# An attention loop's order of work: scores for the row maxima 1.5 steps ahead in place of 2, projections and loads rearranged

## Chip, cores and metric

One Trainium2 chip, one core. The metric is the device time of one execution in microseconds, the median of several runs. The kernel before takes 815.4 us (median of 3 runs, 815.37 to 815.62).

## What is computed

A macaron block on x of shape (8, 512, 128) in float32, 4096 tokens: half a feed-forward block, attention, and half a feed-forward block again. The feed-forward block (`_L0_ffn_ref`: 64 routed experts, the best 8 of a token, 64 places each, and a shared expert) isn't touched by the change. The attention, cut to what matters:

```python
def _L0_attn_ref(x, wq, bq, wk, bk, wv, bv, wo, bo, gamma, beta):
    B, S, E = x.shape            # 8, 512, 128
    H = 16; D = 8
    Q = (x @ wq + bq).reshape(B * H, S, D)
    K = (x @ wk + bk).reshape(B * H, S, D)
    V = (x @ wv + bv).reshape(B * H, S, D)
    scores = jnp.einsum('bqd,bkd->bqk', Q, K) / jnp.sqrt(jnp.float32(D))
    attn = jax.nn.softmax(scores, axis=-1)
    ctx = jnp.einsum('bqk,bkd->bqd', attn, V).reshape(B, S, E)
    out = ctx @ wo + bo + x
    out = layernorm(out) * gamma + beta
    return out

x = x + 0.5 * _L0_ffn_ref(_layernorm(x), ...)
x = x + _L0_attn_ref(_layernorm(x), ...)
x = x + 0.5 * _L0_ffn_ref(_layernorm(x), ...)
```

`Q.reshape(B * H, S, D)` reads rows of x in order, so 32 tokens (a row of 128 values is 16 positions of a head) are one head of 512 positions. A tile of 128 tokens therefore holds 4 whole heads.

## The kernel before

The program is one stream per engine (`block.sync`, `gpsimd`, `vector`, `scalar`, `tensor`), each in the order written, with semaphores between them. It is feed-forward, attention, feed-forward. The attention goes over NT = 32 tiles of 128 tokens; **step n** does tile n, and beside it pieces of later and earlier tiles. In the trace the steps run from about 225 us to 632 us.

What a step n does, by engine:

- **TensorE** (`step`, from line 1755; a loop body for the middle steps and written out for the first and last four). 16 positions `tau` in 4 quarters. Each issues `scores_t` (line 1743), the transposed scores of tile n for one block of keys and one head, into one of two PSUM banks; it waits for the exponential two positions before. At tau 1, 5, 9 and 13 come two calls of `scores` each (lines 1728 and 1730, part p of 8), plain scores of tile n+2 that only serve the row maxima; each waits for the maximum two parts before (`a_mx`). After tau 3, 7, 11 and 15 comes `pv` (line 1752, four heads side by side, each as several matmuls), which is the value product of the quarter before. Between them stand `xT` (line 1687, transpose for tile n+4), `qk` (1692, query and key projection for n+4), `v` (1701, value projection for n+3), `maxT` (1710, transpose of the maxima of n+1) and `proj` (1718, output projection of n-2). These five share PSUM bank 7 in turn: the list `uses` fixes their order, and each waits until the one before it was read.
- **ScalarE** exponentiates each `scores_t` (line 1453) and copies out `xT` (1393, after tau 1), `maxT` (`max_copy`, 1408, after tau 3), the value product (`ctx_copy`, 1414, after tau 3) and `qk` (1400, after tau 7).
- **VectorE** reduces the 8 parts of plain scores of tile n+2 to maxima (`row_max`, 1122), then splits them in two bf16 halves (`max_high` 1126, `max_low` 1130), and between them does `v_copy` (845), the reciprocal of `ctx_div` (1135), `z_add` (1146) and layer norm pieces. Some steps in every four have more of those.
- **GpSimd** multiplies the context by the reciprocal (`context`, 784), splits queries and keys in three bf16 parts (`split`, 759 to 765) and normalises the next tile.
- **SyncE** issues all DMAs of the loop from one queue, in order. `stack_load(n+3)`: 16 DMAs (lines 472 to 484) that bring the parts of tile n+3 back from DRAM as stacks of rows; it waits until those parts have landed in DRAM (`a_pst`) and until step n-1 has issued its last `scores_t`. `max_rows(n+1)` (458): the transposed maxima into two rows of the query stack, which the first `scores_t` of step n+1 needs (`a_mrow`). `ctx_store(n-1)` (498), 256 KB to DRAM. `stack_store(n+4)` (463), 192 KB to DRAM, once `split` is done (`a_parts`). `ctx_load(n-1)` (506): two DMAs that read the context back; it waits until `ctx_store(n-1)` has landed.

The wait that `ctx_load` has, and the wait of a stack load (`wait_each` is the helper at line 96 of the profile):

```python
wait_each(sp, (a_use, use("o", t - 2) + 1 if ... else 0), (a_cst, 16 * t + 16))   # ctx_load(t)
wait_each(sp, (a_ST, 16 * (t - 3)), (a_pst, 16 * t + 16))                         # stack_load(t)
```

Of the kernel before, what the change touches and what calls it, by code (L numbers as in the profile page):

```python
# [15 lines left out]
def macaron_kernel(nc, x_in, wq, bq, wk, bk, wv, bv, wo, bo, gamma, beta,  # L16
# [10 lines left out]
    NT = T // P  # L27
# [24 lines left out]
    NBUF = 4  # L52
    NPB = 8
    AW = 19072
    assert NH * HS == P and C * 2 == P and T % (P * GT) == 0
# [9 lines left out]
    with ExitStack() as ctx:  # L65
# [284 lines left out]
        for n in range(NT + 2):  # L350
            uses += [u for u in (("x", n + 4), ("m", n + 1), ("q", n + 4), ("v", n + 3), ("o", n - 2))
                     if 0 <= u[1] < NT]
# [16 lines left out]
        def _(sp):  # L369
# [84 lines left out]
            def attention():  # L454
# [40 lines left out]
                def ctx_store(t, r):  # L495

                    sp.wait_ge(a_cx, t + 1)
                    sp.dma_start(ctx_dram[r], ctx_r[r % 2]).then_inc(a_cst, 16)
# [28 lines left out]
                def step(n, r, end=NT):  # L527
                    mid = not isinstance(n, int)
                    if mid or n + 3 < end:
                        stack_load(n + 3, (r + 3) % NBUF)  # L530
                    if mid or n + 1 < end:
                        max_rows(n + 1, (r + 1) % NBUF)
                    if mid or n >= 1:
                        ctx_store(n - 1, (r - 1) % NBUF)
                    if mid or n + 4 < end:
                        stack_store(n + 4, r)
                    if mid or n >= 1:
                        ctx_load(n - 1, (r - 1) % NBUF)
                def store_tokens(g):
# [289 lines left out]
        def _(dve):  # L829
# [285 lines left out]
            def attention():  # L1115
# [42 lines left out]
                max_low(0, 0)  # L1158
                for p in range(8):
                    row_max(1, 1, p)  # L1160
                max_high(1, 1)
                max_low(1, 1)

# [42 lines left out]
                for n in range(NT):  # L1206
                    r = n % NBUF
                    at = lambda k: (r + k) % NBUF
                    for p in range(8):
                        if n + 2 < NT:  # L1210
                            row_max(n + 2, at(2), p)
                        if p == 0 and n >= 6 and n % GT == 2:
# [7 lines left out]
                        if p == 3 and n >= 7 and n % GT == 3:  # L1220
                            x_add((n - 7) // GT)
                        if p == 4 and n + 3 < NT:
                            v_copy(n + 3, at(3))
# [4 lines left out]
                        if p == 7 and n >= 7 and n % GT == 3:  # L1228
                            x_var((n - 7) // GT)
                        if n == NT - 2 and p == 1:  # L1230
                            xT_copy(0)
# [7 lines left out]
                        if n == NT - 1 and p == 4:  # L1239
# [3 lines left out]
                            routed(1)  # L1243
                    if n + 2 < NT:
                        max_high(n + 2, at(2))
                        max_low(n + 2, at(2))
                    if n >= 2:
# [39 lines left out]
        def _(act):  # L1287
# [102 lines left out]
            def attention():  # L1390
# [55 lines left out]
                for n in range(NT):  # L1446
                    r = n % NBUF
                    for tau in range(16):
# [5 lines left out]
                        if tau == 1 and n + 4 < NT:  # L1454
                            xT_copy(n + 4, r)
                        if tau == 3 and n + 1 < NT:
                            max_copy(n + 1, (r + 1) % NBUF)
                        if tau == 3 and n >= 1:
                            ctx_copy(n - 1, (r - 1) % NBUF)
                        if tau == 7 and n + 4 < NT:  # L1460
                            qk_copy(n + 4, r)
# [50 lines left out]
        def _(pe):  # L1512
# [165 lines left out]
            def attention():  # L1678
# [77 lines left out]
                def step(n, r, end=NT):  # L1756
                    mid = not isinstance(n, int)
                    at = lambda k: (r + k) % NBUF
                    for tau in range(16):
                        if tau == 0 and (mid or n + 4 < end):  # L1760
                            xT(n + 4, r)
                        if tau == 6 and (mid or n + 4 < end):
                            qk(n + 4, r)
                        if tau == 10 and (mid or n + 3 < end):
                            v(n + 3, at(3))
                        if tau == 14 and (mid or n >= 2):
                            proj(n - 2, at(-2))
                        if not mid and n == NT - 2 and tau == 2:
                            pe.wait_ge(a_mx, 8 * NT)
                            transposes(ffns[1], 0, 0)  # L1770
                        if not mid and (n, tau) in ((NT - 2, 10), (NT - 1, 2), (NT - 1, 10)):
                            g = 2 * (n - (NT - 2)) + tau // 8
                            transposes(ffns[1], g, g % 2)
                            logits(ffns[1], g - 1, (g - 1) % 2)
                        scores_t(n, r, tau)
                        if tau == 3 and (mid or n + 1 < end):
                            maxT(n + 1, at(1))
                        if tau == 3 and (mid or n >= 1):
                            pv(n - 1, at(-1), 3)
                        if tau % 4 == 3 and tau > 3:  # L1780
                            pv(n, r, tau // 4 - 1)
                        if tau % 4 == 1 and (mid or n + 2 < end):
                            scores(n + 2, at(2), tau // 2)
                            scores(n + 2, at(2), tau // 2 + 1)

# [10 lines left out]
                for p in range(8):  # L1796
# [10 lines left out]
                    scores(0, 0, p)  # L1807
                for p in range(8):
                    scores(1, 1, p)
                    if p == 0:  # L1810
                        maxT(0, 0)
# [50 lines left out]
```

## Time and profile before

| | |
|---|---|
| median of 3 runs | 815.4 us (815.37 to 815.62) |
| the profiled execution's own time | 816.08 us |
| its span, first to last instruction | 813.9 us |
| busy in the span: PE, DVE, ACT, POOL | 79%, 74%, 56%, 50% |
| mean granted TensorE clock | 0.833 of full speed |
| step 13, first `scores_t` | 391.94 us |
| step 17, first `scores_t` | 442.69 us |

The clock column of the profile's 40 slices stands at full speed (9) from the thirteenth slice to the thirty-second, which is the attention after its start. The engines' own busy times overlap; SyncE has none, since issuing a DMA isn't counted as work, though its queue is busy with it. The steps come in groups of four: of these the first is 12.4 us long and the other three a little longer, since VectorE has more to do in them.

### The profile page before, as it was taken

Reading aid. Unit: us, or ns where it says so; the run is one execution under the profiler, and the core shown is the slowest. Engines: PE = TensorE matmul, PEld = TensorE weight load, DVE = VectorE, ACT = ScalarE, POOL = GpSimd, SP = SyncE. Lnnn points to the kernel's source line nnn. Section 1 sums busy time; section 2 is a strip of 40 time slices with the busy share of each in tenths; the row PEclk is TensorE's granted clock in tenths of the full one; section 3 lists DMA queues with packets and bytes.
Section 4 is the critical chain, followed back from the end, with each engine's and each line's share of the span. In section 5 each row is a group of like instructions: output and inputs, shape, how many; then the busy total and the mean of one; then the engine's idle time right before and its main releaser. Section 6 shows DMA issues by size and latency. Waiting matters only on the chain.

```text
span 813.9 us, 16314 instructions
## 1 busy us (share of the span) xinstructions
PE 646.0 (79%) x5121; PEld 283.7 (35%) x5121; DVE 599.6 (74%) x1550; ACT 458.5 (56%) x1057; POOL 408.8 (50%) x559
## 2 busy tenths in 40 slices
PE   4896577632699999999999999999999776667760
PEld 3643455421222222222222232222223533445540
DVE  4788834446878989999899998999983779844430
ACT  5653222210158878888888888888888544222220
POOL 5576778854523234344343443434211448578763
PEclk9997755665579999999999999999999568755665
DMA  7898444325544454454545545455421213443334
GB/s 197 235 252 230 94 75 65 52 24 144 96 87 115 100 116 122 104 128 104 123 113 111 122 102 125 111 112 122 104 58 40 68 29 92 110 88 67 60 42 116
DMA packets 242983, 86.66 MB, mean 106 GB/s; under 512 B 169992, under 2 KB 235688, under 8 KB 242856
## 3 DMA queue, kind: packets, MB, share of 16 engines
q1 hardware_dynamic: 226048, 73.05, 37.8%
q0 software_dynamic: 12288, 10.49, 8.7%
q10 hardware_dynamic: 4584, 2.39, 1.0%
q8 instruction: 25, 0.41, 0.2%
q14 instruction: 38, 0.31, 0.1%
HBM read 56.23 MB, written 31.49 MB: 108 GB/s over the span
## 4 chain that ended last, share of the span: by engine, by line
PE 30%; DVE 26%; POOL 13%; issue 13%; ACT 7%; DMA 7%; SPq 1%; ACTq 0%; POOLq 0%; DVEq 0%
DVE arena L1122 14%; PE psum L1752 8%; PE psum L1743 8%; POOL sums L692 7%; ACT arena L1453 4%; DMA sums<-sums_sb,sidx 4%; POOL arena L667 4%; PE psum L1728 4%; DVE arena L1135 3%; PE psum L1533 2%; DMA arena<-dispatch_rows,arena 1%; DVE arena L1130 1%; PE psum L1692 1%; DVE arena L939 1%; PE psum L1550 1%
## 5 line engine op out<-in xcount | busy, mean ns | idle before, releaser
L1122 DVE TENSOR_REDUCE arena<-psum 128x2 f32<-128x1024 f32 x256 | 306.0, 1212 | 36.3 <-PE psum L1730 36.3
L1453 ACT ACTIVATE arena<-psum 128x512 f32<-128x512 f32 x512 | 278.3, 598 | 72.1 <-PE psum L1743 71.2
L1743 PE MATMUL psum<-arena 122*128 122x512 bf16 x512 | 164.4, 387 | 7.0 <-ACT arena L1453 3.5
L1752 PE MATMUL psum<-arena 128*32 128x512 f32 x1024 | 138.2, 610 | 0.0
L692 POOL DMA_INDIRECT sums<-sums_sb,sidx x64 | 102.0, 1594 | 41.2 <-issue 19.4
L1728 PE MATMUL psum<-arena 48*128 48x512 bf16 x256 | 88.4, 400 | 17.0 <-DMA arena<-qk_parts 7.9
L784 POOL TENSOR_TENSOR arena<-arena 128x128 f32<-128x128 f32 x30 | 14.0, 466 | 149.5 <-DVE arena L1135 149.5
L1730 PE MATMUL psum<-arena 48*128 48x512 bf16 x256 | 88.4, 401 | 0.0
L1743 PEld LDWEIGHTS psum<-arena 122*128 122x128 bf16 x512 | 42.7, 100 | 130.1 <-ACT arena L1453 123.5
L667 POOL DMA_INDIRECT arena<-dispatch_rows,arena x64 | 64.1, 1002 | 27.9 <-issue 17.9
L1610 PE MATMUL psum<-ident,arena 128*128 128x128 f32 x64 | 25.0, 413 | 54.6 <-DMA arena<-dispatch_rows,arena 54.5
L1048 DVE COPY sums_sb<-psum 128x256 f32<-128x256 f32 x32 | 13.6, 425 | 65.8 <-PE psum L1654 44.8
L1728 PEld LDWEIGHTS psum<-arena 48*128 48x128 bf16 x256 | 19.2, 94 | 85.5 <-DVE arena L1122 46.3
L1361 ACT ACTIVATE arena<-psum 128x256 f32<-128x256 f32 x32 | 12.3, 384 | 63.1 <-PE psum L1610 63.1
L1367 ACT ACTIVATE arena<-psum 128x192 f32<-128x192 f32 x32 | 10.6, 331 | 65.5 <-PE psum L1620 65.5
L1620 PE MATMUL psum<-wgu_sb,arena 128*32 128x192 f32 x512 | 45.1, 498 | 0.9 <-ACT arena L1361 0.9
L759 POOL CAST arena<-arena 128x256 bf16<-128x256 f32 x30 | 14.6, 487 | 41.8 <-issue 30.0
L1610 PEld LDWEIGHTS psum<-ident,arena 128*128 128x128 f32 x64 | 10.4, 171 | 71.6 <-issue 46.1
L1040 DVE TENSOR_TENSOR arena<-arena,psum 128x192 f32<-128x192 f32 x32 | 11.3, 353 | 27.5 <-ACT arena L1367 27.5
L1752 PEld LDWEIGHTS psum<-arena 128*32 128x32 f32 x1024 | 20.6, 108 | 31.3 <-issue 31.2
L1533 PE MATMUL psum<-rwT,z_sb 128*128 128x64 f32 x128 | 28.3, 397 | 3.8 <-ACT z_sb L1477 3.8
L1135 DVE RECIPROCAL arena<-arena 128x128 f32<-128x128 f32 x32 | 30.1, 942 | 0.0
(152 smaller groups left out, 1178.9 us busy)
## 6 DMA issues: line engine op xcount, KB each, us to landing
ctx<-arena SPq DMA_DIRECT2D x32, 256.0 KB, 2.1
arena<-qk_parts SPq DMA_DIRECT2D x127, 64.0 KB
qk_parts<-arena SPq DMA_DIRECT2D x32, 192.0 KB, 3.8
arena<-qk_parts SPq DMA_DIRECT2D x190, 32.0 KB
arena<-qk_parts SPq DMA_DIRECT2D x63, 96.0 KB
arena<-lists SPq DMA_DIRECT2D x16, 256.0 KB, 3.5
sums<-x_sb SPq DMA_DIRECT2D x16, 256.0 KB, 4.6
arena<-ctx SPq DMA_DIRECT2D x64, 64.0 KB, 2.4
```

Source lines behind the costliest of these rows:

```text
L667: pool.indirect_dma_start(out=gat[k % NGB], out_offset=None, in_=xw_dram[f.p], in_offset=bass.IndirectOffsetOnAxis(ap=gidx[:, k:k + 1], ax ...
L692: pool.indirect_dma_start(out=acc_dram[f.p], in_=sum_r[q % 2][:, j * D:(j + 1) * D], in_offset=None, out_offset=bass.IndirectOffsetOnAxis( ...
L1122: dve.tensor_reduce(mx_r[r % 2][:, p:p + 9:8], src, X, ALU.max).then_inc(a_mx, 1)
L1135: dve.reciprocal(den2_r[r % 2], den2_r[r % 2]).then_inc(a_rc, 1)
L1453: act.activation(p_r[tau % NPB], bank[4 + tau % 2][:, :], ACT.Exp, scale=SCALE).then_inc(a_P, 1)
L1533: ins = pe.matmul(bank[2 + r][:, j * E:(j + 1) * E], xT_all[:, t * P:(t + 1) * P], rwT[:], start=True, stop=True)
L1610: ins = pe.transpose(bank[0][:, j * P:(j + 1) * P], gat[k % NGB][:, 0:D], ident[:])
L1620: ins = pe.matmul(bank[2 + r][i * HC:(i + 1) * HC, j * 2 * F:(j + 1) * 2 * F], gT[r][:, j * P + i * HC:j * P + (i + 1) * HC], wgu_sb[:, e, :],
L1728: pe.matmul(bank[2 * p % 4][:, :], heads(q_st[r], low, g)[:, cols], heads(k_st[r], low, g), start=True, stop=True, tile_position=(0, 0))
L1730: pe.matmul(bank[2 * p % 4 + 1][:, :], heads(q_st[r], high, g)[:, cols], heads(k_st[r], high, g + 2), start=True, stop=True, tile_position ...
L1743: pe.matmul(bank[4 + tau % 2][:, :], keys, heads(q_st[r], rows, g), start=True, stop=True)\
L1752: ins = pe.matmul(bank[6][32 * g:32 * g + 32, :], v_r[r][:, g, kt, :], p_r[(4 * kt + g) % NPB], start=(kt == 0), stop=(kt == 3), tile_posi ...
```

## The change

- TensorE computes plain scores for the maxima 1.5 tiles ahead (`HEAD = 4`): in step n the last four parts of tile n+1 and then the first four of n+2, where it was eight of n+2. The start-up does only four parts of tile 1.
- `qk` moves from tau 6 (inside a quarter) to tau 4 (before the quarter's first `scores_t`); `v` moves from before tau 10 to after tau 7, next to `pv`; `maxT` moves from tau 3 to tau 11. `uses` follows.
- ScalarE: `max_copy` after tau 10 in place of 3, `qk_copy` after tau 4 in place of 7.
- VectorE: the last half of a tile's maxima comes first, `max_high` and `max_low` follow after part 3 of a step; `v_copy` after that.
- SyncE: `ctx_store`, `ctx_load`, `max_rows`, `stack_store` in place of `max_rows`, `ctx_store`, `stack_store`, `ctx_load`.
- In the last two steps the first transposes for the second feed-forward block stand later.

The sizes and the number of instructions in a step stay.

```diff
+    HEAD = 4
...
-            uses += [u for u in (("x", n + 4), ("m", n + 1), ("q", n + 4), ("v", n + 3), ("o", n - 2))
+            uses += [u for u in (("x", n + 4), ("q", n + 4), ("v", n + 3), ("m", n + 1), ("o", n - 2))
...
                     if mid or n + 3 < end:
                         stack_load(n + 3, (r + 3) % NBUF)
+                    if mid or n >= 1:
+                        ctx_store(n - 1, (r - 1) % NBUF)
+                        ctx_load(n - 1, (r - 1) % NBUF)
                     if mid or n + 1 < end:
                         max_rows(n + 1, (r + 1) % NBUF)
-                    if mid or n >= 1:
-                        ctx_store(n - 1, (r - 1) % NBUF)
                     if mid or n + 4 < end:
                         stack_store(n + 4, r)
-                    if mid or n >= 1:
-                        ctx_load(n - 1, (r - 1) % NBUF)
...
-                for p in range(8):
+                for p in range(HEAD):
                     row_max(1, 1, p)
-                max_high(1, 1)
-                max_low(1, 1)
...
                     for p in range(8):
-                        if n + 2 < NT:
-                            row_max(n + 2, at(2), p)
+                        ahead, part = divmod(HEAD + p, 8)
+                        if n + 1 + ahead < NT:
+                            row_max(n + 1 + ahead, at(1 + ahead), part)
+                            if part == 7:
+                                max_high(n + 1 + ahead, at(1 + ahead))
+                                max_low(n + 1 + ahead, at(1 + ahead))
...
-                        if p == 4 and n + 3 < NT:
+                        if p == 3 and n + 3 < NT:
                             v_copy(n + 3, at(3))
...
-                        if tau == 3 and n + 1 < NT:
+                        if tau == 10 and n + 1 < NT:
                             max_copy(n + 1, (r + 1) % NBUF)
...
-                        if tau == 7 and n + 4 < NT:
+                        if tau == 4 and n + 4 < NT:
                             qk_copy(n + 4, r)
...
-                        if tau == 6 and (mid or n + 4 < end):
+                        if tau == 4 and (mid or n + 4 < end):
                             qk(n + 4, r)
-                        if tau == 10 and (mid or n + 3 < end):
-                            v(n + 3, at(3))
...
                         scores_t(n, r, tau)
-                        if tau == 3 and (mid or n + 1 < end):
+                        if tau == 7 and (mid or n + 3 < end):
+                            v(n + 3, at(3))
+                        if tau == 11 and (mid or n + 1 < end):
                             maxT(n + 1, at(1))
...
-                        if tau % 4 == 1 and (mid or n + 2 < end):
-                            scores(n + 2, at(2), tau // 2)
-                            scores(n + 2, at(2), tau // 2 + 1)
+                        if tau % 4 == 1:
+                            ahead, p = divmod(HEAD + tau // 2, 8)
+                            if mid or n + 1 + ahead < end:
+                                scores(n + 1 + ahead, at(1 + ahead), p)
+                                scores(n + 1 + ahead, at(1 + ahead), p + 1)
```

SyncE's queue, the end of one step and the start of the next. Before, from the last load of a stack on (`L482` a key load, `L458` max_rows, `L498` ctx_store, `L463` stack_store, `L506` ctx_load, `L472` the first load of the next stack):

```order
L482 DMA arena<-qk_parts 8x4x512
L458 DMA arena<-arena 2x16x128 [waits a_misc_read]
L498 DMA ctx<-arena 128x512 [waits a_ctx_copied]
L463 DMA qk_parts<-arena 128x24x32 [waits a_parts_ready]
L506 DMA arena<-ctx 128x4x32 [waits a_ctx_stored,a_misc_written]
L506 DMA arena<-ctx 128x4x32
L472 DMA arena<-qk_parts 24x4x512 [waits a_parts_stored,a_scoresT_in_psum]
```

And with the change, whose lines are numbered one higher:

```order
L483 DMA arena<-qk_parts 8x4x512
L499 DMA ctx<-arena 128x512 [waits a_ctx_copied]
L507 DMA arena<-ctx 128x4x32 [waits a_ctx_stored,a_misc_written]
L507 DMA arena<-ctx 128x4x32
L459 DMA arena<-arena 2x16x128 [waits a_misc_read]
L464 DMA qk_parts<-arena 128x24x32 [waits a_parts_ready]
L473 DMA arena<-qk_parts 24x4x512 [waits a_parts_stored,a_scoresT_in_psum]
```

The context's store now has its reload right behind it, and the maxima's rows and the store of the parts stand behind that reload; nothing is left between the parts' store and the load that waits for its landing.

TensorE's second quarter of a step in the loop. Before (`L1743` scores_t, `L1728` and `L1730` plain scores, `L1692` qk, `L1750` and `L1752` pv):

```order
L1743 MATMUL psum<-arena 128x512 [waits a_exp_ready]
L78 REGISTER_ALU
L1728 MATMUL psum<-arena 128x512 [waits a_max_ready]
L1730 MATMUL psum<-arena 128x512
L78 REGISTER_ALU
L1692 MATMUL psum<-arena,wqk_sb 128x128 [waits a_misc_read]
L1692 MATMUL psum<-arena,wqk_sb 128x128
L78 REGISTER_ALU
L1743 MATMUL psum<-arena 128x512 [waits a_exp_ready]
L78 REGISTER_ALU
L1743 MATMUL psum<-arena 128x512 [waits a_exp_ready]
L1750 REGISTER_ALU [waits a_ctx_copied,a_exp_ready]
```

With the change (`L1742` scores_t, `L1727` and `L1729` plain scores, `L1700` v, `L1749` pv's wait):

```order
L1727 MATMUL psum<-arena 128x512 [waits a_max_ready]
L1729 MATMUL psum<-arena 128x512
L79 REGISTER_ALU
L1742 MATMUL psum<-arena 128x512 [waits a_exp_ready]
L79 REGISTER_ALU
L1742 MATMUL psum<-arena 128x512 [waits a_exp_ready]
L79 REGISTER_ALU
L1700 MATMUL psum<-wv_sb,arena 32x32 [waits a_misc_read]
L1700 MATMUL psum<-wv_sb,arena 32x32 x15
L1749 REGISTER_ALU [waits a_ctx_copied,a_exp_ready]
```

The projection no longer stands between the plain scores and the quarter's last two `scores_t`; these now follow the plain scores at once, and the value projection comes after them.

## Rows read from the trace of the kernel before

**Rows 1.** Page, part 1: busy time of each engine over the span.

```profile
PE 646.0 (79%) x5121; PEld 283.7 (35%) x5121; DVE 599.6 (74%) x1550; ACT 458.5 (56%) x1057; POOL 408.8 (50%) x559
```

**Rows 2.** Timeline of PE; columns: start, duration in us, engine, line.

```profile
391.94 0.60 PE L1743 MATMUL psum<-arena 122*128 122x512 bf16 x2
392.47 0.39 PE L1728 MATMUL psum<-arena 48*128 48x512 bf16 x1
...
392.70 0.38 PE L1728 MATMUL psum<-arena 48*128 48x512 bf16 x1
...
393.01 0.88 PE L1743 MATMUL psum<-arena 122*128 122x512 bf16 x2
...
398.52 0.39 PE L1728 MATMUL psum<-arena 48*128 48x512 bf16 x1
...
399.03 0.39 PE L1728 MATMUL psum<-arena 48*128 48x512 bf16 x1
...
442.69 0.38 PE L1743 MATMUL psum<-arena 122*128 122x512 bf16 x1
...
594.37 0.60 PE L1743 MATMUL psum<-arena 122*128 122x512 bf16 x2
```

**Rows 3.** Timeline of SyncE's DMA queue, one step; columns as in rows 2.

```profile
392.18 0.31 SPq L472 DMA_DIRECT2D arena<-qk_parts  x1
...
398.28 0.64 SPq L458 DMA_DIRECT2D arena<-arena  x1
398.95 0.42 SPq L498 DMA_DIRECT2D ctx<-arena  x1
401.06 0.38 SPq L463 DMA_DIRECT2D qk_parts<-arena  x1
401.54 2.14 SPq L506 DMA_DIRECT2D arena<-ctx  x2
...
404.85 0.31 SPq L472 DMA_DIRECT2D arena<-qk_parts  x1
```

**Rows 4.** Waits of SyncE's queue, 300 to 640 us: total us, times, longest.

```profile
SPq L463 <- POOL arena L765: 31.1, 21, 2.7
SPq L96 <- DMA qk_parts<-arena: 23.7, 23, 1.4
SPq L96 <- DMA ctx<-arena: 14.4, 15, 1.7
```

**Rows 5.** Line 463 (stack_store), 300 to 640 us: us from issue to landing.

```profile
DMA to landing us min/median/max: 3.7/3.8/4.3
```

**Rows 6.** Line 498 (ctx_store), same stretch.

```profile
DMA to landing us min/median/max: 2.0/2.1/2.7
```

**Rows 7.** SyncE's queue late in the loop, no stack in flight.

```profile
609.93 0.34 SPq L498 DMA_DIRECT2D ctx<-arena  x1
612.00 0.92 SPq L506 DMA_DIRECT2D arena<-ctx  x2
```

**Rows 8.** SyncE's queue in step 0 and the start of step 1.

```profile
235.12 0.68 SPq L458 DMA_DIRECT2D arena<-arena  x1
...
240.97 0.30 SPq L472 DMA_DIRECT2D arena<-qk_parts  x1
```

**Rows 9.** Timeline of ACT in step 13.

```profile
392.36 1.09 ACT L1453 ACTIVATE arena<-psum 128x512 f32<-128x512 f32 x2 [0.60 <-PE psum L1743]
...
397.85 0.63 ACT L1400 ACTIVATE arena<-psum,bqk_sb 128x128 f32<-128x128 f32 x2
398.41 1.08 ACT L1453 ACTIVATE arena<-psum 128x512 f32<-128x512 f32 x2
```

**Rows 10.** Windows: length, busy us of PE, PEld, DVE, ACT, POOL; PE clock, DMA.

```profile
225.00:235.00 10.00, 9.24 (x32) 2.37 (x30) 6.73 (x8) 5.17 (x12) 0.29 (x1) 0.51 0.45 100
241.00:595.00 354.00, 345.40 (x2909) 101.29 (x2911) 325.08 (x480) 291.39 (x634) 137.94 (x269) 1.00 0.50 114
...
620.00:640.00 20.00, 15.80 (x90) 7.52 (x89) 12.37 (x71) 12.97 (x34) 7.34 (x12) 0.85 0.18 48
```

More of the change, by code:

```diff
@@ L1229, in attention @@
                             x_var((n - 7) // GT)
-                        if n == NT - 2 and p == 1:
+                        if n == NT - 2 and p == 4:
                             xT_copy(0)
@@ L1243, in attention @@
                             routed(1)
-                    if n + 2 < NT:
-                        max_high(n + 2, at(2))
-                        max_low(n + 2, at(2))
                     if n >= 2:
@@ L1761, in step @@
                             xT(n + 4, r)
-                        if tau == 6 and (mid or n + 4 < end):
+                        if tau == 4 and (mid or n + 4 < end):
                             qk(n + 4, r)
-                        if tau == 10 and (mid or n + 3 < end):
-                            v(n + 3, at(3))
                         if tau == 14 and (mid or n >= 2):
                             proj(n - 2, at(-2))
-                        if not mid and n == NT - 2 and tau == 2:
+                        if not mid and n == NT - 2 and tau == 9:
                             pe.wait_ge(a_mx, 8 * NT)
                             transposes(ffns[1], 0, 0)
-                        if not mid and (n, tau) in ((NT - 2, 10), (NT - 1, 2), (NT - 1, 10)):
+                        if not mid and (n, tau) in ((NT - 2, 14), (NT - 1, 2), (NT - 1, 10)):
                             g = 2 * (n - (NT - 2)) + tau // 8
@@ L1807, in attention @@
                     scores(0, 0, p)
-                for p in range(8):
+                for p in range(HEAD):
                     scores(1, 1, p)
```

## Prediction

> **What bounds the kernel now.** I read the page first. PE is busy for 79% of the span and DVE for 74% [rows 1], which doesn't say what limits a step, so I went to the timelines of one stretch, steps 13 to 16. Their first `scores_t` stand at 391.94 and 442.69 [rows 2], so four steps take 50.75 us and one takes 12.69 on average. The whole loop runs with TensorE at its full clock, 2.4 GHz over 241 to 595 us [rows 10].
>
> In PE's timeline the reader is to see two small stalls. The first `scores_t` of a quarter starts at 391.94, its exponential only at 392.36, and a pair of exponentials takes 1.09 [rows 9]. The third `scores_t` therefore can't start before about 393.0, and the fourth follows the second exponential at 393.5, which is why the row at 393.01 lasts 0.88 where a pair takes 0.60 [rows 2]. The other stall is DVE's: two parts of plain scores start 0.51 apart (398.52 and 399.03), where a part takes 0.23 (392.47 to 392.70 [rows 2]), so PE waited 0.28 for a maximum. Steps with more work on DVE are longer than 12.42, the length of step 13, and 12.69 - 12.42 = 0.27 is what that costs on average. All that a perfect removal of the maxima's wait could give is so 0.28 + 0.27 = 0.55 us a step.
>
> Then the queue that has no busy time on the page, SyncE's [rows 3]. It issues 16 stack loads from 392.18 on, the maxima's rows at 398.28, the context's store at 398.95, then waits for `split` and stores the parts at 401.06, reloads the context at 401.54 (2.14 long), and issues the next stack load at 404.85, which is when the parts' store has landed. Over 300 to 640 us this last wait occurs 23 times for 23.7 us [rows 4]. One turn of the queue is 12.67 here, against a step of 12.69: **the queue is already as long as the step**, with one free place in it, the wait for `split` (31.1 us over 21 times [rows 4], 1.5 a turn). In the present order two landings lie under other things: the context's 2.1 under that wait for `split`, and 2.5 of the parts' 3.8 under the reload.
>
> **The change, part by part.**
>
> *SyncE's order.* No DMA is added or removed, but each landing now stands bare. One turn:
> - 16 stack loads: 392.18 to 398.28 [rows 3], 6.10.
> - `ctx_store` to the start of `ctx_load`, which now waits for its landing right behind it: 2.07 where nothing else is in flight [rows 7]; the landing has a median of 2.1 and reaches 2.7 [rows 6]. I take 2.15, the median and a short gap.
> - `ctx_load`: 0.92 when the queue is quiet [rows 7], against 2.14 behind the parts' store [rows 3]. It is quiet now. With the gap 0.96.
> - `max_rows`: 398.28 to 398.95, 0.67.
> - `stack_store` to the next stack load: 401.06 to 404.85, 3.79; landings are 3.7 to 4.3 [rows 5].
>
> The sum is 6.10 + 2.15 + 0.96 + 0.67 + 3.79 = 13.67; I use 13.7. The low end is 13.5 (2.07, and 3.7 for the landing), the high end about 14.7 (2.7 and 4.3). I stay near the low end, since the parts' store will find only the two small reloads ahead of it, and stores that followed another transfer by a second or more landed in the median time. What is ready is ready: `split` ends about 9 us into a step (401.06 - 391.94), the store now comes 9.9 into the turn, and the copy of the maxima after tau 10 comes about 9 us into a step that began before the turn did.
>
> The Trainium skill, "DMA: Bandwidth & Descriptors", section "Anatomy of one DMA", fits a DMA's time as 2.0 us and its bytes over 436 KB per us, measured for GpSimd's path. By it the 192 KB store would take 2.45 and the 256 KB one 2.6, and the turn 12.8. The trace disagrees for the 192 KB store, which lands in 3.8 [rows 5]; its runs are of 64 bytes.
>
> *Who waits for the queue.* `max_rows(n+1)` stands 9.2 us into the turn (6.10 + 2.15 + 0.96) and the first `scores_t` of step n+1 waits for its landing. Its landing isn't listed; the nearest rows are landings of 2.0 to 2.1 [rows 6, 7], and I take 2.1. So step n+1 starts 11.3 after turn n began. Turn n+1 begins 13.7 after turn n, and nothing in it waits for the engines: from the first turns on, a step takes a turn, 13.7, also the steps in which DVE has more to do. The stacks themselves aren't late; they have half a step more.
>
> *The total.* Turn 1 begins at 240.97 now [rows 8]. With the change `split` for tile 4 is earlier, since step 0 no longer waits behind four parts of scores, so the store follows `max_rows` (235.12 + 0.67 = 235.79), and turn 1 begins at 235.79 + 3.79 = 239.6. There are 27 turns with a store in them (n from 1 to 27). Step 29 starts at 239.6 + 27 x 13.7 + 11.3 = 620.8 in place of 594.37 [rows 2]: 26.4 us later. For the last three steps and the second feed-forward block I take no difference: they have no stack to load, and the transposes that move a few positions there are followed by work that waits for other things. **The sum is +26.4 us.** It is made against the profiled execution, 816.08 by its own time (span 813.9 and 2.2 around it), which is 0.7 above the median. Against the median it is 815.4 + 26.4 = 841.8, and I say 842.
>
> *PE's and ACT's order.* Beside that the engines' own path gets longer, but less. In the second quarter `qk` stood between the plain scores and the third `scores_t` and covered the exponential's 1.06 us (0.41 to its start, 0.60 and a gap). Now `qk_copy` (0.56 in ACT's stream: 397.85 to 398.41 [rows 9]) falls between the quarter's first and second exponential. The fourth `scores_t` can start 0.42 + 0.49 + 0.56 + 0.60 + 0.05 = 2.12 after the first, where its place in PE's order is 0.27 x 3 + 0.45 = 1.26 (three `scores_t` at half of 392.47 - 391.94 each, two parts of scores at 0.23): a stall of 0.86. In the third quarter the same holds without the copy, 1.56 against 1.26: 0.3, which `v` covered. Of the 0.55 for DVE's waits I let 0.5 go, since the reciprocal and the extra pieces get no longer and the maxima have half a tile more room. So 0.86 + 0.3 - 0.5 = +0.66 a step, to 13.35, below the turn of 13.7. It hides under the queue; were the queue short, it would be the cost.
>
> **Rivals.**
> - *The queue doesn't bind, the engines' order does.* It would be so if the landings came faster when nothing follows them. Step 13.35: 27 x 0.66 = 17.8 later, less about 1 at the start, 832. Against it: a turn of 13.35 needs every piece below its least row. By the Trainium skill's fit above (a turn of 12.8) this is what would happen. Chance 0.11.
> - *Faster.* If SyncE's turn also hid (below 12.2) and the exponential's stalls were covered by `pv`, only the gain would be left: 0.55 a step, 27 x 0.55 = 15 less, 800; halved, 808. The point from which it decides is a turn of 12.69. For it: 15 waits for the context's landing are short already [rows 4]. Against it: the two landings alone are 5.9 of a turn now. Chance 0.03, and 0.02 that both halves cancel within 0.2%.
> - *The clock falls.* PE will stand idle for some 1 to 2 us at the start of a step. In 620 to 640 us it was busy for 15.80 of 20 us and the clock went down to 0.85 on average; at 225 to 235 it was 0.51, that is 1.2 GHz, with PE busy for 9.24 of 10 us [rows 10]. At half clock a step's 11 us of matmuls would be longer than any turn; step by step that is 5 us or more each, and three such steps 15 more, 857. The Trainium skill, "TensorE: Matmul & The Clock Gate", section "HAM oscillation", says that DMA waits within a matmul loop can take the clock down again and again. By that rule it would be 857 or more. Here PE stays busy for over 80% of each step with short gaps only. Chance 0.04.
>
> **The numbers.** The forecast, a step of one turn of 13.5 to 14.2, has 0.80: 836 to 856. The range 833 to 856 takes in the turn's likely values and touches the engines-only case. A measurement of this kernel tells about 0.2% from no change. Slower by more: 0.80 + 0.11 + 0.04 = 0.95; same 0.02; faster 0.03.
>
> **What would show it.** Right: first `scores_t` of steps 13.7 apart with no difference between the four kinds of step; SyncE's queue never waiting for `split`, waiting 1.7 a turn for the context's landing and 3.4 for the parts'; PE's wait before a step's first `scores_t` put down to the DMA of the maxima's rows; the clock at 1.00 throughout. Wrong: steps of four different lengths, waits for `split` still there, or the next stack load starting less than 3.7 after the store.

## The result, and the profile after

The changed kernel takes 860.0 us (median of 4 runs, 854.0 to 860.8) against 815.51 us for the kernel before on the same chip: a ratio of 1.0512, 95% interval 1.0462 to 1.0561. The direction and the mechanism of the prediction hold; the time lies above the range (833 to 856). The profiled execution took 854.0 us by its own time (span 852.0), so the rows below explain 38 of the 44.5 us; the other executions are told of with the first experiment. Two more executions on record took 853.8 and 859.07: they lie near 854 or near 860.

The chain that ended last, as shares of the span by engine, of the kernel before:

```profile
PE 30%; DVE 26%; POOL 13%; issue 13%; ACT 7%; DMA 7%; SPq 1%; ACTq 0%; POOLq 0%; DVEq 0%
```

and of the changed kernel:

```profile
DMA 23%; SPq 19%; issue 14%; PE 13%; DVE 13%; POOL 13%; ACT 4%; POOLq 0%; ACTq 0%; DVEq 0%
DMA qk_parts<-arena 10%; POOL sums L692 7%; DMA ctx<-arena 5%; SPq L473 5%; SPq L483 4%; POOL arena L667 4%; DVE arena L1122 3%; DMA sums<-sums_sb,sidx 3%; SPq L485 3%; SPq L475 3%; PE psum L1751 3%; PE psum L1742 3%; SPq L507 2%; ACT arena L1452 2%; PE psum L1532 2%
```

TensorE and VectorE had 56% of the chain and now have 26%; SyncE's queue and the DMAs had 8% and now have 42%. The busy time of PE barely moved, which is why the first part of the page says nothing of this loss:

```profile
PE 646.1 (76%) x5121; PEld 280.6 (33%) x5121; DVE 610.0 (72%) x1550; ACT 466.6 (55%) x1057; POOL 406.1 (48%) x559
```

It answers to [rows 1]. Next, one turn of SyncE's queue in the changed kernel (timeline: start, duration, engine, line), which answers to [rows 3]:

```profile
479.48 0.31 SPq L473 DMA_DIRECT2D arena<-qk_parts  x1
...
485.58 0.35 SPq L499 DMA_DIRECT2D ctx<-arena  x1
487.70 0.93 SPq L507 DMA_DIRECT2D arena<-ctx  x2
488.67 0.63 SPq L459 DMA_DIRECT2D arena<-arena  x1
489.34 0.41 SPq L464 DMA_DIRECT2D qk_parts<-arena  x1
493.17 0.31 SPq L473 DMA_DIRECT2D arena<-qk_parts  x1
```

The loads take 6.10, the context's store to its reload 2.12, the reload 0.97, the maxima's rows 0.67, the parts' store to the next load 3.83: 13.69 in all, where the prediction had 13.67. The waits of SyncE's queue over 300 to 615 us (total, times, longest):

```profile
SPq L97 <- DMA qk_parts<-arena: 65.6, 22, 3.6
SPq L97 <- DMA ctx<-arena: 41.6, 23, 2.8
SPq L459 <- DVE z_sb L1146: 1.1, 2, 0.6
```

The wait for `split`, 31.1 us in [rows 4], is gone, and the two landings have grown from 23.7 and 14.4 to 65.6 and 41.6. TensorE's own rows show who waits at the other end. The first is the start of step 13, the second of step 17, the others of steps 18 and 29 (in brackets the idle time ahead and what ended it):

```profile
406.98 0.39 PE L1742 MATMUL psum<-arena 122*128 122x512 bf16 x1
...
463.35 0.60 PE L1742 MATMUL psum<-arena 122*128 122x512 bf16 x2
...
477.00 0.60 PE L1742 MATMUL psum<-arena 122*128 122x512 bf16 x2 [0.30 <-DMA arena<-arena]
...
630.27 0.64 PE L1742 MATMUL psum<-arena 122*128 122x512 bf16 x2 [2.29 <-DMA arena<-arena]
```

`DMA arena<-arena` is the transfer of the maxima's rows. Steps 13 to 16 last 56.37 us, 14.09 each, against 12.69 [rows 2]. The steps aren't alike, as they were forecast to be: they last from 13.4 to 15.1. One in four takes about 14.03, longer than a quiet turn, and a shorter one follows.

### The profile page after: what moved, and what is told of

Its sections match the earlier page's. It is cut to its first block, busy times and chain, and to the rows that moved or that the text cites. A ratio compares the mean times of both kernels' runs of the same rounds, so it can differ in the third digit from the quotient of the medians.

```text
span 852.0 us, 16314 instructions
## 1 busy us (share of the span) xinstructions
PE 646.1 (76%) x5121; PEld 280.6 (33%) x5121; DVE 610.0 (72%) x1550; ACT 466.6 (55%) x1057; POOL 406.1 (48%) x559
## 4 chain that ended last, share of the span: by engine, by line
DMA 23%; SPq 19%; issue 14%; PE 13%; DVE 13%; POOL 13%; ACT 4%; POOLq 0%; ACTq 0%; DVEq 0%
DMA qk_parts<-arena 10%; POOL sums L692 7%; DMA ctx<-arena 5%; SPq L473 5%; SPq L483 4%; POOL arena L667 4%; DVE arena L1122 3%; DMA sums<-sums_sb,sidx 3%; SPq L485 3%; SPq L475 3%; PE psum L1751 3%; PE psum L1742 3%; SPq L507 2%; ACT arena L1452 2%; PE psum L1532 2%
## 5 line engine op out<-in xcount | busy, mean ns | idle before, releaser
L1452 ACT ACTIVATE arena<-psum 128x512 f32<-128x512 f32 x512 | 283.6, 597 | 96.2 <-PE psum L1742 95.8
L1742 PE MATMUL psum<-arena 122*128 122x512 bf16 x512 | 172.7, 389 | 38.9 <-ACT arena L1452 18.6
L1742 PEld LDWEIGHTS psum<-arena 122*128 122x128 bf16 x512 | 43.2, 98 | 175.0 <-ACT arena L1452 151.3
L1727 PE MATMUL psum<-arena 48*128 48x512 bf16 x256 | 85.6, 397 | 12.6 <-DMA arena<-qk_parts 7.1
L1729 PE MATMUL psum<-arena 48*128 48x512 bf16 x256 | 85.6, 397 | 0.0
L1609 PE MATMUL psum<-ident,arena 128*128 128x128 f32 x64 | 24.7, 409 | 59.3 <-DMA arena<-dispatch_rows,arena 59.2
L1727 PEld LDWEIGHTS psum<-arena 48*128 48x128 bf16 x256 | 17.6, 94 | 76.5 <-issue 34.4
L1686 PE MATMUL psum<-ident,arena 128*128 128x128 f32 x32 | 11.1, 348 | 24.9 <-POOL arena L739 22.2
L1532 PEld LDWEIGHTS psum<-rwT,z_sb 128*128 128x128 f32 x128 | 26.0, 302 | 9.0 <-ACT z_sb L1476 5.1
```

The source lines that it names most:

```text
L1452: act.activation(p_r[tau % NPB], bank[4 + tau % 2][:, :], ACT.Exp, scale=SCALE).then_inc(a_P, 1)
L1532: ins = pe.matmul(bank[2 + r][:, j * E:(j + 1) * E], xT_all[:, t * P:(t + 1) * P], rwT[:], start=True, stop=True)
L1609: ins = pe.transpose(bank[0][:, j * P:(j + 1) * P], gat[k % NGB][:, 0:D], ident[:])
L1727: pe.matmul(bank[2 * p % 4][:, :], heads(q_st[r], low, g)[:, cols], heads(k_st[r], low, g), start=True, stop=True, tile_position=(0, 0))
L1729: pe.matmul(bank[2 * p % 4 + 1][:, :], heads(q_st[r], high, g)[:, cols], heads(k_st[r], high, g + 2), start=True, stop=True, tile_position ...
L1742: pe.matmul(bank[4 + tau % 2][:, :], keys, heads(q_st[r], rows, g), start=True, stop=True)\
```

## The experiments

Two theories were to be told apart. **Queue**: SyncE's turn, with both landings bare, sets the step. **Engines' order**: the projections' new places and the look-ahead cost the time, and the queue is hidden. They were tested in both directions, the change with the old queue order and the kernel before with the new one. The ratios are against the kernel before in the same set of runs: 816.61 us (7 runs) for after_again, old_queue, new_queue and ahead_alone, 815.43 us (17 runs, on another chip) for the others.

### after_again: the changed kernel once more

> The changed kernel once more, for its spread and a second profile. Queue theory (SyncE's turn of 16 loads, context store and its landing, context reload, maxima's rows, parts' store and its landing sets the step): the quiet turns are again 13.7 us, and the mean turn lies above 14.03 where the time is near 860, since more landings come late; the time is 854 to 861. Clock theory: the extra 6 us of such an execution stand in steps in which TensorE's granted clock is below 1.00, with turns as long as before.

It took 856.29 us (854.35 to 859.09), a ratio of 1.0476 (1.0458 to 1.0493). Its profiled execution took 859.09, 5.1 more than the one above. The distance from the first stack load of turn 1 to that of turn 2 is the clearest place. Timeline of SyncE's queue:

```profile
238.97 0.30 SPq L473 DMA_DIRECT2D arena<-qk_parts  x1
...
245.06 0.78 SPq L499 DMA_DIRECT2D ctx<-arena  x1
249.75 0.93 SPq L507 DMA_DIRECT2D arena<-ctx  x2
250.72 0.63 SPq L459 DMA_DIRECT2D arena<-arena  x1
251.39 0.41 SPq L464 DMA_DIRECT2D qk_parts<-arena  x1
255.21 0.31 SPq L473 DMA_DIRECT2D arena<-qk_parts  x1
```

This turn is 16.24 long, since the context's store took 4.7 to land in place of 2.1. Over the loop the landings of that store are (min, median, max)

```profile
DMA to landing us min/median/max: 2.0/2.0/4.7
```

and those of the parts' store

```profile
DMA to landing us min/median/max: 3.7/3.8/5.2
```

The medians are within 0.1 of those in [rows 5, 6]; the longest are longer. The 27 turns from the first load of turn 1 to that of turn 28 (238.97 to 622.39 here, 239.47 to 618.20 in the execution of 854.0) average 14.20 and 14.03, and 27 x 0.17 = 4.6 of the 5.1 us. Of that the context's landings make 2.5, the loads 1.5 and the parts' landings 0.8. The quiet turns are 13.65 to 13.74 in both. The clock's share is small: its mean over 240 to 345 us was 0.97 here and 1.00 in the other.

### old_queue: the change with SyncE's old order

```diff
-                    if mid or n >= 1:
-                        ctx_store(n - 1, (r - 1) % NBUF)
-                        ctx_load(n - 1, (r - 1) % NBUF)
                     if mid or n + 1 < end:
                         max_rows(n + 1, (r + 1) % NBUF)
+                    if mid or n >= 1:
+                        ctx_store(n - 1, (r - 1) % NBUF)
                     if mid or n + 4 < end:
                         stack_store(n + 4, r)
+                    if mid or n >= 1:
+                        ctx_load(n - 1, (r - 1) % NBUF)
```

> The change with SyncE's old order (max_rows, ctx_store, stack_store, ctx_load), the engines' order as changed. Queue theory: the queue's part goes and the engines' own order is left, 13.2 to 13.4 us a step against 12.69: 27 x 0.6 = +16, so 829 to 835. Rival, the engines' order alone makes the loss: no change against the changed kernel, 854 to 860. Rival, the queue alone makes it and the engines' order is free or gains: 800 to 816.

834.10 us (833.87 to 836.03), a ratio of 1.0219 (1.0202 to 1.0236). Steps 13 to 16 begin and end here:

```profile
396.57 0.60 PE L1743 MATMUL psum<-arena 122*128 122x512 bf16 x2
...
450.61 0.38 PE L1743 MATMUL psum<-arena 122*128 122x512 bf16 x1
```

54.04 us, 13.51 a step. So the queue's order is worth 22 us against 856.3 on this chip, and the engines' order 17.5 us that the queue had hidden. The spread of the runs is 2.2 us where it was 4.7, but that tells nothing of the landings: it is 4.1 in ahead_alone and 4.3 in reload_last, where they are hidden too.

### new_queue: the kernel before with SyncE's new order alone

```diff
                     if mid or n + 3 < end:
                         stack_load(n + 3, (r + 3) % NBUF)
+                    if mid or n >= 1:
+                        ctx_store(n - 1, (r - 1) % NBUF)
+                        ctx_load(n - 1, (r - 1) % NBUF)
                     if mid or n + 1 < end:
                         max_rows(n + 1, (r + 1) % NBUF)
-                    if mid or n >= 1:
-                        ctx_store(n - 1, (r - 1) % NBUF)
                     if mid or n + 4 < end:
                         stack_store(n + 4, r)
-                    if mid or n >= 1:
-                        ctx_load(n - 1, (r - 1) % NBUF)
```

> The kernel before with SyncE's new order alone (ctx_store, ctx_load, max_rows, stack_store), the engines as before. Queue theory: turns of 13.7 when quiet, 14.0 on average as in the changed kernel, step 29 begins at 241 + 27 x 14.0 + 11.3 = 630 in place of 594, so 849 to 858. Rival, the engines' order makes the loss: within 2 us of 815.5.

855.89 us (854.59 to 858.28), a ratio of 1.0474 (1.0456 to 1.0491), the same as the whole change in the same set of runs (1.0476). TensorE's waits at the start of steps 13 and 17 have the same cause:

```profile
412.81 0.39 PE L1742 MATMUL psum<-arena 122*128 122x512 bf16 x1 [0.83 <-DMA arena<-arena]
...
468.49 0.39 PE L1742 MATMUL psum<-arena 122*128 122x512 bf16 x1 [0.79 <-DMA arena<-arena]
```

This settles it: two calls moved ahead in SyncE's program, on otherwise unchanged engines, make the whole loss. The 27 turns average 14.09. The time was forecast well, the sum less so: turn 1 began at 243.55, 2.6 later than expected, and step 29 at 636.97 in place of 630, in an execution of 858.28 us.

### reload_last: only the context's reload moved back

```diff
                     if mid or n >= 1:
                         ctx_store(n - 1, (r - 1) % NBUF)
-                        ctx_load(n - 1, (r - 1) % NBUF)
                     if mid or n + 1 < end:
                         max_rows(n + 1, (r + 1) % NBUF)
                     if mid or n + 4 < end:
                         stack_store(n + 4, r)
+                    if mid or n >= 1:
+                        ctx_load(n - 1, (r - 1) % NBUF)
```

> The change with ctx_load moved behind stack_store (queue order ctx_store, max_rows, stack_store, ctx_load); everything else as changed. Queue theory: the landing of the context lies under the maxima's rows and the wait for split, the landing of the parts under the reload, so the turn fits in the step again and the time is that of old_queue, 831 to 837, 20 or more below the changed kernel. Rival, what costs is that the maxima's rows come late or behind any other transfer: little change, 850 or more.

834.07 us (832.45 to 836.79), a ratio of 1.0237 (1.0200 to 1.0274): that of old_queue. Of the two moved calls it is the reload, directly behind its own store, that carries the loss. The waits over 300 to 615 us show that the maxima's rows now wait for ScalarE's copy. They aren't late for that: over 300 to 580 us no wait of TensorE for their transfer is listed, and steps 13 to 16 last 54.06 us, as in old_queue (54.04).

```profile
SPq L459 <- ACT arena L1408: 50.6, 23, 3.0
...
SPq L97 <- DMA qk_parts<-arena: 25.1, 23, 1.8
```

What the reload's place is worth can be read from one turn:

```profile
487.40 0.41 SPq L464 DMA_DIRECT2D qk_parts<-arena  x1
487.92 2.13 SPq L507 DMA_DIRECT2D arena<-ctx  x2
491.25 0.31 SPq L473 DMA_DIRECT2D arena<-qk_parts  x1
```

From the parts' store to the next load it is 3.85 with the reload in between, 3.79 in the kernel before [rows 3] and 3.83 in the changed one without it. The new order doesn't lengthen this stretch; it takes the reload (0.97) out of it, and it adds the wait for the context's landing (2.12 less 0.42 for the issue, 1.70). In step 13 of the kernel before the turn of 12.67 held a wait of 1.69 for `split` (2.11 from the context's store to the parts' store, less 0.42), so its own length was 11.0, and 11.0 + 0.97 + 1.70 = 13.7.

### qk_alone: one part of the engines' order, in the kernel before

```diff
-                        if tau == 7 and n + 4 < NT:
+                        if tau == 4 and n + 4 < NT:
                             qk_copy(n + 4, r)
...
-                        if tau == 6 and (mid or n + 4 < end):
+                        if tau == 4 and (mid or n + 4 < end):
                             qk(n + 4, r)
```

> The kernel before with qk alone moved to tau 4 and its copy after the exponential 4. By the prediction's term (fourth scores_t of the quarter 0.86 late) 27 x 0.86 = +23, 838 to 841. If the late fourth scores_t gives DVE the time that PE waited for it before (0.28 a step), 27 x 0.58 = +16, near 832. If the exponentials are covered by the value product all the same: 815 to 818.

830.03 us (826.04 to 831.04), a ratio of 1.0165 (1.0125 to 1.0206). The second expectation is the nearest. TensorE's second quarter in step 13:

```profile
400.99 0.60 PE L1743 MATMUL psum<-arena 122*128 122x512 bf16 x2
...
402.06 0.39 PE L1743 MATMUL psum<-arena 122*128 122x512 bf16 x1
403.06 0.39 PE L1743 MATMUL psum<-arena 122*128 122x512 bf16 x1 [0.61 <-ACT arena L1453]
...
404.92 0.39 PE L1728 MATMUL psum<-arena 48*128 48x512 bf16 x1
...
405.17 0.39 PE L1728 MATMUL psum<-arena 48*128 48x512 bf16 x1
```

The fourth `scores_t` starts 2.07 after the first (the prediction had 2.12), and the two parts of scores behind it are 0.25 apart in place of 0.51 [rows 2]: the late `scores_t` gave VectorE the time. Step 13 (397.55 to 410.50) is 12.95 long against 12.42: the stall of 0.81 less the 0.26 given back.

### ahead_alone: the look-ahead of 1.5 steps with the projections at their old places

```diff
-                        if tau == 4 and n + 4 < NT:
+                        if tau == 7 and n + 4 < NT:
                             qk_copy(n + 4, r)
...
-                        if tau == 4 and (mid or n + 4 < end):
+                        if tau == 6 and (mid or n + 4 < end):
                             qk(n + 4, r)
+                        if tau == 10 and (mid or n + 3 < end):
+                            v(n + 3, at(3))
...
-                        if tau == 7 and (mid or n + 3 < end):
-                            v(n + 3, at(3))
```

(against old_queue)

> The look-ahead of 1.5 steps with the old queue order and with qk (before the seventh scores_t, copied after the eighth) and v (before the eleventh) back at their places. If the uncovered exponentials next to the plain scores are what the engines' order costs (0.86 + 0.3 us a step by the prediction), this is 12 us or more below old_queue, 805 to 822. If the look-ahead itself costs, it is within 3 us of old_queue.

823.28 us (822.25 to 826.37), a ratio of 1.0092 (1.0070 to 1.0114), 10.8 below old_queue and so a little short of the 12 expected. So the uncovered exponentials are most of the engines' part but not all of it; the look-ahead, with the places of `maxT`, of its copy, of `v_copy` and of the last transposes, which weren't tried apart, still costs 6.7 us against the kernel before. The timeline of step 13 shows how. TensorE's parts of scores in its third and fourth quarters:

```profile
400.62 0.39 PE L1728 MATMUL psum<-arena 48*128 48x512 bf16 x1
...
401.12 0.39 PE L1728 MATMUL psum<-arena 48*128 48x512 bf16 x1
...
403.93 0.39 PE L1728 MATMUL psum<-arena 48*128 48x512 bf16 x1
...
404.59 0.39 PE L1728 MATMUL psum<-arena 48*128 48x512 bf16 x1 [0.27 <-DVE arena L1123]
```

and VectorE between them:

```profile
399.05 0.94 DVE L1136 RECIPROCAL arena<-arena 128x128 f32<-128x128 f32 x1
399.90 1.16 DVE L1123 TENSOR_REDUCE arena<-psum 128x2 f32<-128x1024 f32 x1
401.10 0.17 DVE L1127 CAST arena<-arena 128x16 bf16<-128x16 f32 x1
401.31 0.57 DVE L1131 TENSOR_TENSOR arena<-arena 128x16 bf16<-128x16 f32 x1
401.98 0.29 DVE L846 TENSOR_TENSOR arena<-psum,bv_sb 128x128 f32<-128x128 f32 x1
```

The wait of 0.28 (0.51 - 0.23) is there as before, and a second one of 0.43 has come. The halves of the maxima stood behind the last maximum of a step and now stand in its middle, one maximum behind the reciprocal, while TensorE waits for the maxima that follow.

### ahead_early_recip and before_early_recip: the reciprocal one part earlier

Both have the same edit, on ahead_alone and on the kernel before:

```diff
-                        if p == 2 and n >= 2:
+                        if p == 1 and n >= 2:
                             ctx_div(n - 2, at(-2))
```

> ahead_alone with the context's reciprocal one part earlier on DVE (after the second maximum of a step in place of the third). Theory: with the look-ahead of 1.5 steps the reciprocal (0.94), the two halves of the maxima and v_copy stand close together in the middle of the step, and PE waits for the maxima there (0.28 and 0.44 us in step 13 of ahead_alone). Moved, most of it goes: 27 x 0.3 to 0.7 = 8 to 19 less than ahead_alone, 805 to 815. Rival, the waits are the halves' own: no change, 821 to 826.

814.61 us (812.79 to 817.52, 10 runs), a ratio of 0.9989 (0.9969 to 1.0010): by the ratios 1.0% (8 us) below ahead_alone, and no different from the kernel before. In step 13 the first of the two waits is gone and the second has stayed: the parts of scores start at 398.13 and 398.35 in the third quarter, and at 401.15 and 401.81 in the fourth:

```profile
401.81 0.39 PE L1728 MATMUL psum<-arena 48*128 48x512 bf16 x1 [0.27 <-DVE arena L1123]
```

and VectorE ahead of that:

```profile
399.20 0.29 DVE L846 TENSOR_TENSOR arena<-psum,bv_sb 128x128 f32<-128x128 f32 x1 [0.83 <-PE psum L1701]
```

So the theory holds for the first wait and not for the second. VectorE's row names a likely cause of that one: VectorE, done with the halves, stood idle for 0.83 us until the value projection came, though a part of scores had been ready since 398.5. `v_copy` had moved one part forward and `v` not. Its place wasn't tried by itself. Steps 13 to 16 last 50.79 us, in ahead_alone 51.95.

> The kernel before with the reciprocal one part earlier, nothing else. PE's wait for a maximum after the reciprocal is 0.28 us in a step of 12.42, and the longer steps wait more. Theory: the reciprocal then falls where PE does the value product and the maxima aren't awaited, 27 x 0.28 = 7.6 less or a little more, 805 to 809. Rival, the wait only moves to another maximum: 814 to 818.

809.97 us (808.33 to 810.75, 6 runs), a ratio of 0.9929 (0.9902 to 0.9956). **This kernel beats both.** The two parts of scores that were 0.51 apart now follow each other (timeline of PE, step 14):

```profile
406.80 0.39 PE L1728 MATMUL psum<-arena 48*128 48x512 bf16 x1
...
407.02 0.38 PE L1728 MATMUL psum<-arena 48*128 48x512 bf16 x1
```

and VectorE has an idle 0.30 us ahead of a maximum where TensorE used to wait:

```profile
403.71 0.94 DVE L1135 RECIPROCAL arena<-arena 128x128 f32<-128x128 f32 x1
404.57 2.29 DVE L1122 TENSOR_REDUCE arena<-psum 128x2 f32<-128x1024 f32 x2
...
407.23 1.23 DVE L1122 TENSOR_REDUCE arena<-psum 128x2 f32<-128x1024 f32 x1 [0.30 <-PE psum L1730]
```

Step 13 starts at 388.09 and step 14 at 400.21, a step of 12.12 in place of 12.42. Two of the four kinds of step gain 0.3 each and the other two, with the most layer-norm work on VectorE, nothing: the four from 13 to 16 last 50.16 us (388.09 to 438.25) against 50.75. Over steps 1 to 26 that is 4.4 us of the profiled execution's 6.1 (span 807.8 against 813.9). Of the rest, 1.8 stands ahead of step 1, where the edit does nothing (`ctx_div` begins at n = 2), so by this pair of traces the gain is nearer the weak end of its interval.

## Why the prediction was right in kind and wrong in size

**The forecast case happened.** The queue's order alone takes the kernel before to 1.0474 (new_queue), and with the old order the change costs 1.0219 (old_queue), which the prediction had as its engines-only rival at 832 (measured 834.1). A quiet turn is 13.69, with the 192 KB store landing in 3.8. The fit of the Trainium skill ("DMA: Bandwidth & Descriptors", "Anatomy of one DMA"), which would have made the turn 12.8 and so led to that rival, isn't borne out by this trace: the 192 KB store takes 3.8, where the estimate by the fit is 2.45, and the 256 KB one 2.1, where it is 2.6. Three of the signs that the prediction named are there, the vanished wait for `split`, the waits for the two landings (1.8 and 3.0 each time, where it had 1.7 and 3.4) and the maxima's rows ahead of a step. Steps 13.7 apart without a difference aren't.

**The step that failed is the turn's length.** "The sum is 6.10 + 2.15 + 0.96 + 0.67 + 3.79 = 13.67; I use 13.7" and "I stay near the low end". 13.7 is the quiet turn, and 27 turns aren't all quiet. In the same order the means are 6.30 + 2.22 + 0.98 + 0.67 + 3.85, a turn of 14.03, in the execution of 854.0 us, and 6.35 + 2.32 + 0.97 + 0.67 + 3.88, a turn of 14.20, in that of 859.1. The term that is most off is the first, the 16 loads: 0.20 and 0.25 of the 0.36 and 0.53 missing. The context's landing comes next (0.07 and 0.17); the parts' landing, for which the prediction gave its reason to stay low, is off least for its size (0.06 and 0.09). The terms were taken from single quiet turns and medians, and what a chain of waits adds up to is the means. A slow load or a late landing counts in full, since nothing in the new order hides it, and no early one gives anything back.

The trace of the kernel before had said it. Its 16 loads take 6.29 on average over the same 27 turns, and 6.8 to 7.1 in turns 4 to 6, where a single issue is long:

```profile
280.78 1.37 SPq L474 DMA_DIRECT2D arena<-qk_parts  x1
```

I had seen such a stretch (7.0 us, near 280 us) and left it out, since there it lay under other waits. In the changed kernel the loads take 6.4 to 7.4 in turns 3 to 7, and in after_again's turn at 299.58 a single issue lasts 1.25 us in place of 0.30. Why these issues are long isn't known. A landing of the context's store of 2.7 [rows 6] and one of the parts' of 4.3 [rows 5] were in the kernel before too, where they were hidden. In the changed kernel the context's go up to 3.2:

```profile
DMA to landing us min/median/max: 2.0/2.1/3.2
```

**The account of the 38 us in the profiled execution.** Step 29 was to start at 620.8 and started at 630.27: 9.5 late, of which 27 x 0.33 = 8.9 is the turns' mean, and the rest one more late landing: turn 28's reload started 3.00 after its store (624.29 to 627.29) in place of 2.1, and PE was idle for 2.29 ahead of that step. "For the last three steps I take no difference" missed 2.4: steps 29 and 30 begin at 630.27 and end at

```profile
656.91 0.61 PE L1742 MATMUL psum<-arena 122*128 122x512 bf16 x2
```

26.64 us for 24.21 before (594.37 to 618.58). Half of it is the order: in old_queue step 30, the one with the moved transposes, lasts from 623.46 to 636.91, 13.45 against 12.33. The other half is TensorE's clock, below. The 26.4 forecast, 9.5 and 2.4 make 38.3, and the span grew by 38.1. The median lies 6.0 above the profiled execution, and no trace of that set shows why. after_again's profiled execution, 5.1 above, had it in the turns; that the others did too is likely and not shown. With turns of 14.20 and the 2.4 the prediction's sum gives 841.8 + 13.5 + 2.4 = 857.7.

**The engines' part was nearly right as a sum and wrong in a piece.** It was put at +0.66 a step, 13.35; old_queue has 13.51. The exponential's stall was well sized (2.07 against 2.12). "Of the 0.55 for DVE's waits I let 0.5 go, since ... the maxima have half a tile more room" was wrong: in ahead_alone none of the waits went and a second one came. The wait is for the maximum two parts before, whatever tile it belongs to, and the halves now stand in the middle, where VectorE already had the reciprocal.

**The clock rival's time came near, its mechanism only in small.** It had 857 or more at a chance of 0.04. In the profiled execution the mean granted clock was 1.00 over the loop (241 to 628 us). Once it fell, behind the 2.29 us in which PE was idle ahead of step 29; the last three columns are clock, DMA share and GB/s:

```profile
628.00:630.00 2.00, 0.00 (x0) 0.00 (x0) 0.55 (x2) 0.00 (x0) 0.00 (x0) 1.00 0.44 70
631.00:632.00 1.00, 1.00 (x5) 0.13 (x2) 0.50 (x1) 0.79 (x2) 0.00 (x0) 0.50 0.00 0
```

From 631 to 634 us it was at the lower level, 0.50 or 1.2 GHz, and from 634.5 to 640 at 1.00, 2.4 GHz, again. The step took 13.19 where old_queue's took 11.93 (611.53 to 623.46), 1.3 us and not 15. Within the loop a slower step can hide under the queue's turn: in new_queue the mean clock was 0.95 over 245 to 345 us, with turns of 14.09 on average and the same time as after_again's.

## What to carry to other kernels

A queue that issues DMAs in order is an engine like the others, though the page gives it no busy time: add up its turn, issues and landings, without its waits for other engines, and compare the sum with the step before moving anything on it. With those waits a turn is always as long as the step (12.67 and 12.69 here), which tells nothing; without them it was 11.0. A store and the load that reads it back belong apart, with other issues between them; put next to each other, each turn pays the whole landing, and one such pair, with its reload taken out of the other landing, made a 12.7 us step into one of 14. And where issues and landings stand bare in a chain, size each by its mean over all turns, slow ones included, not by a quiet turn or a median.

## What the runs showed that I had not expected

- The landing of one and the same 256 KB store has a median of 2.0 to 2.1 us and goes up to 4.7, and that of the 192 KB one from 3.7 to 5.2, at about 100 GB/s of traffic. Between the two traced executions of the changed kernel landings make 3.3 of the 5.1 us. What makes the spread of 4 to 6 us that kernels with hidden landings also have (812.99 to 818.81 for the kernel before in one set) isn't known.
- The length of one idle stretch of TensorE ahead of a step doesn't tell alone whether the clock falls. In the changed kernel 1.65 us (to 279.67) was followed by a granted clock of 1.00 and 2.29 us (to 630.27) by 0.50; in new_queue 1.65 us (to 285.12) and 2.31 us (to 314.43) were followed by 0.50, and 1.96 us (to 441.12) by 1.00.
- A reciprocal of 0.94 us, moved by one place on an engine whose work stays the same, is worth 5.5 us (815.43 to 809.97), of which the traces place 4.4 in the loop. Why the two kinds of step with more layer-norm work don't gain was not tried.
